# The turn of the block scales ahead of the tails of gate and up, and its copy ahead of the second silu

## The reference, cut to what matters

```python
def fp4_quant_dequant(x):
    xb = x.reshape(shape[:-1] + (shape[-1] // 16, 16))
    scale = jnp.maximum(jnp.max(jnp.abs(xb), axis=-1, keepdims=True) / 6.0, 1e-12)
    idx = jnp.searchsorted(_MID, jnp.abs(xb / scale))
    return (_GRID[idx] * jnp.sign(xb / scale) * scale).reshape(shape)

x = _layernorm(x + attention(x))
gate, y = fp4_linear(x, w_gate), fp4_linear(x, w_up)      # 256 -> 704, twice
h = jax.nn.silu(gate) * y
x = _layernorm(x + fp4_linear(h, w_down))                 # 704 -> 256
```

## Time and profile before

| | |
|---|---|
| median of three runs | 687.15 us (686.71 to 689.19) |
| the profiled execution | 687.63 us |
| its span, first to last instruction | 685.6 us |
| TensorE, GpSimd, VectorE, ScalarE busy | 97%, 89%, 83%, 76% of the span |
| mean granted TensorE clock | 0.997 of full speed |

### The profile page before, as it was taken

One profiled execution on the slowest core, in us unless ns is written; L12 is line 12 of the kernel. 1 busy time (PEld: TensorE's weight loads), 2 busy tenths in 40 slices (PEclk: granted clock), 3 DMA queues, 4 the chain that ended last, 5 costly groups with the idle time before them and its releaser, 6 DMA issues.

```text
span 685.6 us, 14440 instructions
## 1 busy us (share of the span) xinstructions
PE 667.9 (97%) x4216; PEld 584.8 (85%) x4216; DVE 570.2 (83%) x1438; ACT 524.4 (76%) x1037; POOL 612.0 (89%) x925
## 2 busy tenths in 40 slices
PE   7999999999999899999999999999999999999995
PEld 6888888888887789888989998999989989999994
DVE  5678778776779888899899999999988899988774
ACT  4677777775778667788888889888898888887663
POOL 3988898998979998898999999999999999998766
PEclk9999999999999999999999999999999999999998
DMA  8543344444311111444757555665557664500001
GB/s 271 193 139 132 120 134 130 139 139 154 124 63 32 34 60 47 95 96 97 143 116 160 129 128 115 124 163 131 126 98 119 112 145 95 110 17 16 32 17 46
DMA packets 51099, 74.39 MB, mean 109 GB/s; under 512 B 26380, under 2 KB 31054, under 8 KB 51022
## 3 DMA queue, kind: packets, MB, share of 16 engines
q1 hardware_dynamic: 50602, 73.35, 42.8%
q10 hardware_dynamic: 420, 0.13, 0.1%
HBM read 41.75 MB, written 25.89 MB: 99 GB/s over the span
## 4 chain that ended last, share of the span: by engine, by line
PE 69%; POOL 13%; issue 9%; DMA 3%; DVE 3%; ACT 2%; SPq 0%; POOLq 0%; DVEq 0%; ACTq 0%
PE banks L477 18%; PE banks L478 17%; PE banks L479 17%; PE banks L618 6%; POOL arena L1335 4%; PE banks L648 3%; POOL arena L1302 3%; PE banks L540 3%; DMA resid<-scales_scratch 2%; PE banks L488 2%; POOL arena L1305 1%; POOL lnbuf L1311 1%; PE banks L501 1%; POOL arena L1324 1%; DMA resid<-in_L_attn_Wv_dram 1%
## 5 line engine op out<-in xcount | busy, mean ns | idle before, releaser
L477 PE MATMUL banks<-wgu_hi,actT_lo 128*128 128x512 f32 (+1 forms) x384 | 145.5, 379 | 0.3 <-DVE actT_lo L1105 0.2
L478 PE MATMUL banks<-wgu_lo,actT_hi 128*128 128x512 f32 (+1 forms) x384 | 143.6, 374 | 0.0
L479 PE MATMUL banks<-wgu_hi,actT_hi 128*128 128x512 f32 (+1 forms) x384 | 143.2, 373 | 0.0
L477 PE MATMUL banks<-wd_hi,actT_lo 128*128 128x256 f32 x320 | 100.3, 313 | 0.1
L1302 POOL TENSOR_TENSOR arena<-arena 128x704 f32<-128x704 f32 x64 | 89.6, 1401 | 10.8 <-DVE arena L1090 10.8
L479 PE MATMUL banks<-wd_hi,actT_hi 128*128 128x256 f32 x320 | 90.3, 282 | 0.0
L478 PE MATMUL banks<-wd_lo,actT_hi 128*128 128x256 f32 x320 | 90.2, 282 | 0.0
L477 PEld LDWEIGHTS banks<-wgu_hi,actT_lo 128*128 128x128 f32 x384 | 72.4, 188 | 11.9 <-DVE actT_lo L1105 1.5
L479 PEld LDWEIGHTS banks<-wgu_hi,actT_hi 128*128 128x128 f32 x384 | 72.1, 188 | 10.5
L478 PEld LDWEIGHTS banks<-wgu_lo,actT_hi 128*128 128x128 f32 x384 | 72.4, 189 | 9.6
L1335 POOL TENSOR_TENSOR arena<-arena,s 128x960 f32<-128x960 f16 (+2 forms) x46 | 75.9, 1649 | 0.0
(11 more groups left out here) (146 smaller groups left out, 1966.3 us busy)
## 6 DMA issues: line engine op xcount, KB each, us to landing
xs<-x_plus_scratch SPq DMA_DIRECT2D x32, 512.0 KB, 4.2
x_plus_scratch<-xs SPq DMA_DIRECT2D x24, 512.0 KB, 2.9
resid<-scales_scratch SPq DMA_DIRECT2D x22, 512.0 KB
arena<-in_L_attn_x_dram SPq DMA_DIRECT2D x32, 256.0 KB, 3.6
out_dram<-arena SPq DMA_DIRECT2D x32, 256.0 KB, 6.1
x_plus_scratch<-arena SPq DMA_DIRECT2D x4, 512.0 KB, 2.9
x_plus_scratch<-resid SPq DMA_DIRECT2D x4, 512.0 KB, 3.4
resid<-in_L_attn_x_dram SPq DMA_DIRECT2D x4, 256.0 KB, 6.2
```

The costliest lines, as they stand in the source:

```text
L477: nc.tensor.matmul(dst, sl, mh, start=(k == 0), stop=False, skip_group_check=shared)
L478: nc.tensor.matmul(dst, sh, ml, start=False, stop=False, skip_group_check=shared)
L479: last = nc.tensor.matmul(dst, sh, mh, start=False, stop=(ended and k == n - 1), skip_group_check=shared)
```

## The change

Two calls are moved, and nothing else. On TensorE the turn of the scales stands ahead of the tails of gate and up in the same step. On ScalarE its copy stands ahead of the second silu. The waits inside the two functions are the same.

```diff
@@ TensorE, step(t)
                     gate_up(t, 1 if t > 0 else 2)
                 if joint(t + 1) and not late(t):
                     turn(t + 1)
+                if by_dma(t + 3):
+                    scales_turn(t + 3)
                 if there(t):
                     gate_up(t, 2 if t > 0 else 1)
                 if joint(t + 1) and late(t) and not by_dma(t + 1):
                     turn(t + 1)
-                if by_dma(t + 3):
-                    scales_turn(t + 3)
                 if there(t + 9):
                     attend(t + 9)
@@ ScalarE, step(t)
                 if there(t + 1 - LAG) and h_with_x(t + 1):
                     high_h(t + 1)
+                if by_dma(t + 3):
+                    scales_copy(t + 3)
                 if there(t):
                     silu(t, 1)
                 if there(t + 1) and late(t):
                     high_x(t + 1)
-                if by_dma(t + 3):
-                    scales_copy(t + 3)
                 if joint(t + 3) and not pair(t + 33):
                     to_f16(t + 3)
```

## The result

The changed kernel takes 701.21 us (median of 6 runs, 700.16 to 704.22), the kernel before took 687.12 us beside it (6 runs, 686.59 to 689.51). The ratio is 1.018 [1.015, 1.021]: slower, by more than the forecast of 693.3 us, and 0.2 us above its range. The profiled execution took 701.25 us, its span is 699.4 us.

The account below looks back on a forecast made before the run. TensorE's pair and the start of the last but one L1324 were taken as the bound; 19 pairs of 14.48 + 0.40 us add 6.2 us to 687.63, giving 693.8, less 0.48 for the median: 693.3 us, range 685 to 701.

Parts of the forecast that it names:

- The moved steps: Turn at s + 2.75, copy 1.29 us earlier, L453 at s + 6.42, L1324 0.95 to 0.14 us ahead of s.
- s: Start of the first gate matmul of the step with the scales, from which the prediction counts times in a pair.
- The 0.09 us for the turn on TensorE: First tail after the moved fp32 turn takes 0.26 us, not 0.17; 0.09 us a pair, bounds 0 and 0.09.
- I take 0.40: Stall of TensorE's L648 per pair, VectorE's cut waiting for GpSimd's L1335: 0.40 us, bounds 0 and about 1.1.
- the 19 pairs of the sum: Pairs from L1324 at 301.94 to L1324 at 578.49: 276.55 us before, forecast 282.7 us, 6.2 us more.
- the formula x + 1.10: Stall of L648 per pair if L1324 starts at s + x; x -1.03 to -0.62 gives 0.07 to 0.48 us.
- GpSimd carries this to the end: Claim that the 6.2 us added between the two L1324 starts reach the kernel's end through GpSimd.
- the row of 2.04 us: Profile row at 294.47: the cut took 2.04 us, ending 0.28 us behind L1335; read as a full wait.
- No clash: Rival: L1335 starts behind the cut, or VectorE and GpSimd can share; 685.8 us, chance 0.22.
- Hidden: Rival: GpSimd does not use the earlier transfers, something else lands last; 687 to 689 us, chance 0.15.
- the full clash: Rival: every pair stalls like the early one, 1.1 us; about 20 us more, 707 us, chance 0.08.

Follow-up runs that it names:

- hold_gpsimd: The changed kernel with GpSimd's L1324 also waiting for the residual sum L1129 of its step: 686.58 us, 0.995 of the kernel before.
- xagain_on_scalar: The changed kernel with L1002 taken off VectorE and a 16-column copy on ScalarE in its place, two biases left out: 692.8 us, 1.006.
- cut_even_rows: The changed kernel with the cut of a DMA tile split into two instructions of 14 and 2 rows: 723.48 us, 1.051.
- the halves: The kernel before with one move each: the turn alone ahead of the tails, 689.52 us; the copy alone ahead of the second silu, 692.33 us.
- the changed kernel with the wait: The changed kernel with L1324 also waiting for the residual sum of its step, run twice: 686.58 us and 686.36 us.
- the split in the kernel before: The kernel before with the cut of a DMA tile split into 13 and 3 rows: 688.41 us, 1.000.

## Why the prediction was right in its mechanism and too small in its size

**The moved steps: right.** Turn, copy and L453 stand where they were put, L1324 starts 1.31 to 0.30 us ahead of s in the steady stretch, and the cut falls into L1335.

**The 0.09 us for the turn on TensorE: fell.** The first tail still takes 0.26 us after the turn (442.30 to 442.56), but it starts only 0.03 us behind it, and the unhindered pair of hold_gpsimd is 14.39 us, as before. The term is 0, its lower bound.

**The stall, "I take 0.40": the term that was mis-sized, because L1002 was left out of it.** Over the 19 pairs of the sum, a pair takes 0.73 us more than 14.39 us, where the prediction had 0.49 us with the turn. It has two parts. In the 11 pairs without L1002 the excess is 0.26 us, less than predicted, and here the working holds: the earlier L1324 starts, the earlier L1335 ends and the less the cut waits, as the formula x + 1.10 has it. An L1324 at s - 0.33 was followed by an excess of 0.70 us (formula 0.77), one at s - 0.75 by 0.29 us (0.35), one at s - 1.30 by 0.04 us (below 0); in all 11 pairs the formula, taken as 0 where it is negative, is within 0.1 us. L1324 started 0.82 us ahead of s on average there, where the working had 0.71, as the codes landed a little sooner than the 5.40 us after L436 that it had. The view of their tile gives, from issue to landing, after and before,

```profile
DMA to landing us min/median/max: 3.7/5.1/5.8
...
DMA to landing us min/median/max: 5.3/6.6/7.4
```

In the 8 pairs with L1002 the excess is 1.38 us, which the formula doesn't give. The prediction asked which instruction falls into L1335 and named one. It didn't look for the others that VectorE runs while GpSimd multiplies; this one has 8 records, and the pairs it delays have 11.0 of the 13.9 us of excess. Not all of that is its own: without it on VectorE the 19 pairs were 5.6 us shorter (xagain_on_scalar).

**"GpSimd carries this to the end": fell.** The sum ran from one L1324 to another, and in the kernel before, the second of them stood 1.26 us behind its s and the first 0.69 us ahead of it: 1.95 us of shift that the change takes back. That counts only if the end hangs on GpSimd. The chain of waits of the changed kernel stays on TensorE's transposes 45 us longer than in the earlier trace rows:

```profile
601.65 1.06 PE banks L648 x8
...
616.12 0.87 PE banks L648 x8
...
623.70 0.87 PE banks L648 x8
629.64 0.75 POOL lnbuf L1311
631.45 1.75 POOL arena L1335
```

and from the last s it is 108.3 to 109.2 us to the end in every kernel but cut_even_rows (109.6), whatever x is. The sum should have gone from s to s. Put together: 6.2 us forecast, 1.95 us for the shift, 4.6 us for the stall (8 x 0.89 more, 11 x 0.23 less), which is 12.7 us for these 19 pairs as measured; the first two pairs gave back 1.1 us, and 2.1 us lie outside. The kernel with the cut's wait and without L1002 on VectorE (xagain_on_scalar) has 281.7 us in the 19 pairs, where the prediction's sum had 282.7: what the prediction saw was sized well, in part by luck, since that sum held 0.09 us a pair (1.7 us) for TensorE that wasn't there. What it didn't see was L1002.

**The rivals.** "No clash" would have needed L1324 later than s + 0.15; hold_gpsimd makes it so, and takes 686.6 us where that rival said 685.8. "Hidden" fell, since GpSimd did use the earlier transfers. A stall of the size of the full clash (1.1 us) or more is what the pairs with L1002 (1.38 us) and the pairs of cut_even_rows (1.3 us and more) show.

**The page that was weighed.** The prediction held one page of the Trainium skill against the row of 2.04 us, and the row won. Another page says it outright: by the Trainium skill (SBUF — State Buffer, "SBUF: two separate sides") the port pair that VectorE and GpSimd share is an exclusive lock, not a split of bandwidth; who starts first has it for its whole instruction, and the other blocks. It names VectorE instructions with two SBUF inputs as well, and L1002 is one (1.75 us on average instead of 0.91). The runs agree: 3 columns that take 0.10 us took up to 1.61 us and ended with GpSimd's instruction. By the Trainium skill (VectorE: DVE Perf Modes, "Mode 2×_2P") that two-port mode needs an outermost dimension that is even, or odd and equal on both sides. The shapes on VectorE agree. The trace records the cut as rows of 64 on the side that is read and as one run on the side that is written: 16 rows and 1024, 14 and 896, 2 and 128 are even and wait, 13 and 832, 3 and 192 are neither both even nor equal and don't wait, and these pay for it with 0.74 us instead of 0.42 us. The copy of 3 columns has 3 on both sides, and waits.

**Left open.** Why the kernel before leaves the meeting after three pairs, and the halves after 6 and 10, is open: the counts were read from single profiles. That this makes the spread of their times (685.2 to 694.2 us for the kernel before over all its runs, against 684.9 to 687.4 us for the changed kernel with the wait) is argued, not shown; the split in the kernel before narrowed the spread and left the median where it was.

## What to carry to other kernels

Before an instruction is made earlier on GpSimd, list everything that VectorE runs at the new time, with both kinds of instruction that waited here (a sum of two operands in SBUF, and a copy or scalar operation of one operand between SBUF tiles in a shape like the whole cut's), not just the largest; each of them could wait for nearly the whole of a GpSimd instruction, whatever its own size. Where the follower isn't the bound, a wait that holds it back (here 0.85 us behind s) was worth more than a start that is as early as possible (686.6 against 701.2 us). Make a sum between two points of the engine that sets the end, not between two points of one that follows it.

## What the runs showed of the hardware

- A VectorE copy of 128x3 elements took 0.10 us by itself and 1.35 to 1.61 us in the six of eight cases in which it fell into a GpSimd multiply; a sum of 128x16 took 0.11 and 1.39 to 1.98 us, one of 128x512 0.63 and 1.87 to 2.28 us. The end was set by the other engine: they ended 0.02 to 0.03 us (the two small ones) and 0.55 us (128x512) behind GpSimd's instruction, and the cut of 128x1024 uint16 0.28 us behind it.
- The cut in 13 and 3 rows takes 0.74 us instead of 0.42 us and runs beside a GpSimd multiply of 1.79 us without lengthening either.
- GpSimd gives way too: L1302, 1.40 us by itself, took 1.85 us where VectorE's L1002 was still running at its start.
- The DMA transpose of the codes landed after 5.1 us (median) in the changed kernel, where L453 goes out 2.30 us ahead of it (567.44 to 569.74), and after 6.6 us before. What makes the difference was not tried.
